# New turns for the head steps and group ends of the experts phase

## The reference

```python
h = x + _gqa(_rmsnorm(x, attn_norm_w), wq, wk, wv, wo)
out = h + _moe(_rmsnorm(h, ffn_norm_w), gate_w, expert_w)
# _moe: logits = t @ gate_w.T; w, sel = top_k(logits, 2); w = softmax(w)
#       comb = sum(w * one_hot(sel)); out = sum over 8 experts of comb[:, e] * (t @ expert_w[e].T)
# and behind it: x = x + _layernorm(out)
```

## Time and profile before

| | us |
|---|---|
| median of 3 runs | 711.88 (710.86 to 712.08) |
| profiled execution, in all | 706.54 |
| its span | 704.8 |
| experts phase in it | 586.5 to 704.8 |

### The profile page before, as it was taken

One profiled execution on the slowest core, in us unless ns is written; L12 is line 12 of the kernel. 1 busy time (PEld: TensorE's weight loads), 2 busy tenths in 40 slices (PEclk: granted clock), 3 DMA queues, 4 the chain that ended last, 5 costly groups with the idle time before them and its releaser, 6 DMA issues. The chain is left out here.

```text
span 704.8 us, 11736 instructions
## 1 busy us (share of the span) xinstructions
PE 560.1 (79%) x3810; PEld 312.0 (44%) x3810; DVE 524.4 (74%) x2234; ACT 359.0 (51%) x738; POOL 269.7 (38%) x467
## 2 busy tenths in 40 slices
PE   1966488568867998597999999999998988997670
PEld 1865377466656665112233333333334544553230
DVE  6599999442564777598899999999980552695986
ACT  5841045400202667102687887878877543445534
POOL 2001108700004467301445454454544542645564
PEclk9997565557995999655799999999999987998795
DMA  8000000000000184300111121111200000000001
GB/s 306 1 1 1 0 1 1 0 1 0 1 1 1 57 245 147 112 0 7 29 35 36 29 62 30 35 35 29 63 2 7 1 1 2 0 15 16 15 30 45
DMA packets 17579, 24.76 MB, mean 35 GB/s; under 512 B 3246, under 2 KB 14014, under 8 KB 17342
## 3 DMA queue, kind: packets, MB, share of 16 engines
q1 hardware_dynamic: 16942, 21.91, 10.1%
q10 hardware_dynamic: 576, 2.10, 0.9%
HBM read 13.65 MB, written 10.35 MB: 34 GB/s over the span
## 5 line engine op out<-in xcount | busy, mean ns | idle before, releaser
L1422 DVE CUSTOM_DVE_ANT_0 d_masked_S<-d_pS,d_wide_mask 128x512 bf16<-128x512 f32 (+3 forms) x512 | 217.0, 485 | 15.2 <-PE d_pS L1546 10.2
L1520 ACT ACTIVATE d_P<-d_pT 128x768 f32<-128x768 f32 (+1 forms) x192 | 165.9, 882 | 62.8 <-PE d_pT L1546 61.3
L1390 POOL TENSOR_SCALAR_AFFINE_SELECT d_P<-d_P 128x256 f32<-128x256 f32 x256 | 102.6, 415 | 133.9 <-ACT d_P L1520 133.9
L1546 PE MATMUL d_pS<-Ks,Qs 48*128 48x512 bf16 (+3 forms) x512 | 109.9, 332 | 19.7 <-DVE d_mx L1422 9.0
L1546 PE MATMUL d_pO<-d_P,V 128*32 128x512 f32 (+3 forms) x1024 | 99.2, 463 | 1.4 <-POOL d_P L1390 0.9
L1546 PE MATMUL d_pT<-Qs,Ks 51*128 51x512 bf16 (+3 forms) x512 | 72.3, 310 | 2.0 <-ACT d_mT L1490 2.0
L1546 PEld LDWEIGHTS d_pS<-Ks,Qs 48*128 48x128 bf16 x512 | 34.8, 97 | 72.1 <-DVE d_mx L1422 62.2
L1895 PE MATMUL e_PE<-gate_expT,w_qkvT 128*128 128x512 f32 x96 | 52.4, 698 | 7.1 <-DVE e_T L1764 3.3
L1546 PEld LDWEIGHTS d_pT<-Qs,Ks 51*128 51x128 bf16 x512 | 20.7, 94 | 73.8 <-ACT d_P L1520 42.3
L1422 DVE DVE_READ_ACCUMULATOR2_ANT d_mx<- 128x1 f32 x512 | 42.3, 83 | 0.0
L1739 POOL TENSOR_TENSOR e_T<-e_T 128x512 f32<-128x512 f32 x16 | 20.3, 1267 | 44.2 <-ACT e_T L1872 28.5
(11 more groups left out here) (312 smaller groups left out, 1092.3 us busy)
## 6 DMA issues: line engine op xcount, KB each, us to landing
Qs<-q_stack SPq DMA_DIRECT2D x32, 192.0 KB, 3.0
q_stack<-Qp SPq DMA_DIRECT2D x8, 384.0 KB, 2.6
X<-in_x_dram ACTq DMA_DIRECT2D x4, 512.0 KB, 6.3
q_stack<-Qp SPq DMA_DIRECT2D x8, 256.0 KB, 2.5
out_dram<-e_moe SPq DMA_DIRECT2D x8, 256.0 KB, 2.0
w_qkvT<-in_w_qkvT_dram SPq DMA_DIRECT2D x1, 1536.0 KB
Ks<-k_stack SPq DMA_DIRECT2D x32, 48.0 KB, 3.2
q_stack<-Qp SPq DMA_DIRECT2D x8, 128.0 KB, 2.1
```

The lines of the kernel that those rows point to most:

```text
L1390: last = nc.gpsimd.affine_select(out=view, in_=view, compare_op=ALU.is_ge, fill=0.0, base=0, pattern=[[0, 2], [1, 128]], channel_multiplie ...
L1422: last = nc.vector.tensor_tensor_reduce(out=out_[:, at:at + w], in0=src[:, at:at + w], in1=wide_mask[:, 512 - w:512], scale=1.0, scalar=LO ...
L1520: nc.scalar.activation(P[pair % 4][:, :, P_AT[unit]:P_AT[unit] + w], pT[(3 * pair + unit) % 2][:, :, 0:w], ACT.Exp, scale=float(HD4) ** -0 ...
L1546: return nc.tensor.matmul(out, lhsT, rhs, start=start, stop=stop)
```

## The change

The turns of the phase are set anew. Each of the two chunks gets a place of its own (1 and 12) in the place of eight turns a chunk, and the head steps get other distances. In turns counted from the phase's start:

| step | chunk 2 before, after | chunk 3 before, after |
|---|---|---|
| transposes of the attention | 2, 1 | 10, 12 |
| projection | 3, 4 | 11, 15 |
| residual | 4, 4 | 12, 15 |
| mean square | 5, 5 | 13, 16 |
| inverse root | 6, 6 | 14, 17 |
| transposes of h | 6, 7 | 14, 18 |
| gate | 7, 10 | 15, 21 |
| choice | 9, 9 | 17, 20 |
| exponential | 10, 11 | 18, 22 |
| weights | 11, 12 | 19, 23 |

At a group's end total and deviation stay in turns 4g + 6 and 4g + 7. VectorE's shift, now called `scalars`, goes from 4g + 8 to 4g + 9, ScalarE's normalising from 4g + 8 to 4g + 11, GpSimd's finish from 4g + 10 to 4g + 13. No instruction is added or taken away.

```diff
-        PE_STEPS = {-14: "attention_by_channel", -13: "project", -10: "h_by_channel", -9: "gate"}
-        DVE_STEPS = {-12: "residual", -7: "choose", -5: "weigh"}
-        ACT_STEPS = {-14: "attention_by_channel", -11: "mean_square", -10: "h_by_channel", -6: "exp_difference"}
-        POOL_STEPS = {-10: "inverse_root"}
-        GROUP_TURNS = {"total": 6, "deviation": 7, "normalise": 8, "finish": 10}
-        TURNS = range(TILES + 7)
+        HEAD_AT = {2: 1, 3: 12}
+        PE_STEPS = {0: "attention_by_channel", 3: "project", 6: "h_by_channel", 9: "gate"}
+        DVE_STEPS = {3: "residual", 8: "choose", 11: "weigh"}
+        ACT_STEPS = {0: "attention_by_channel", 4: "mean_square", 6: "h_by_channel", 10: "exp_difference"}
+        POOL_STEPS = {5: "inverse_root"}
+        GROUP_TURNS = {"total": 6, "deviation": 7, "scalars": 9, "normalise": 11, "finish": 13}
+        TURNS = range(TILES + 10)
 
         def due(u, steps):
 
-            return [(steps[u - CT * c], c) for c in chunks if u - CT * c in steps and (c >= EARLY or u >= CT * c)]
+            return [(steps[u - at], c) for c, at in HEAD_AT.items() if u - at in steps]
...
-                def normalise(g):
+                def scalars(g):
...
-                    for g in group_due(u, "normalise"):
-                        normalise(g)
+                    for g in group_due(u, "scalars"):
+                        scalars(g)
                         if g == LAST:
                             dve.wait_ge(sm["out"], LAST)
                             finish_last()
```

## The result

| | before | after |
|---|---|---|
| median of the runs, us | 711.41 (710.86 to 712.08) | 701.85 (700.78 to 704.04) |
| span of the profiled execution | 704.8 | 700.6 |
| experts phase in it (start, length) | 586.51, 118.3 | 590.91, 109.7 |

The ratio of the times is 0.9869, 95% interval 0.9842 to 0.9896: 1.3% faster, 9.6 us between the medians. The forecast was 705.0 us.

A forecast was written before the change was run, and what follows sets the result against it. It took the bound to alternate: a chain through ScalarE's wait where heads run, almost VectorE alone in the tail. Tile 30 at 679.9, work ending 694.9 and a 3.0 store gave span 697.9; 711.88 - 6.9 = 705.0 us, range 699.5 to 710.0.

The forecast's parts named there:

- The walk: Experts phase in the new order, laid out on VectorE's scale starts with prices and waits; span 697.9, 6.9 us less.
- the blocking between tiles 16 and 24: VectorE held by GpSimd in this stretch: pair 2.3, choosing 1.0, weighing 1.2, two totals 0.5, so 5.0 us.
- the pair of group 2: VectorE's two small scalar instructions for that group, claimed blocked beside GpSimd's root and a finish, 2.3 us.
- both readings of the root: Whether GpSimd's root blocks VectorE at group 2's pair: taken as blocked; the opposite reading would be 1.6 us lower.
- the reason for the gain before tile 16: Normalising two turns behind its scalars never waits and chunk 3's steps hang on nothing late; 8.1 us won.
- The group in the tail: Steady state after the head steps: 10.6 us a group against 11.4, with ScalarE's wait gone and VectorE full.
- The 3.7 us at tile 4: Projection now follows tile 4, so VectorE's scale of it comes 3.7 us earlier, 599.0 instead of 602.76.
- the waits at the residual and at tile 6: VectorE waits 1.6 us for chunk 2's projection, then 1.3 us while TensorE does tiles 5 and 6.
- the longer end: After the last statistics, group 6's normalising and finish follow the last deviation: 4.6 us where before took 2.6.
- A: VectorE's scalar pairs: none of three blocked, or each once only; 3 to 6 us more, about 700.5; chance 0.18.
- B: Gates one turn behind choosing, TensorE at 1.2 GHz adding 3.6 us at chunk 2, 1.2 at chunk 3: 709.8; chance 0.14.
- C: TensorE's clock held at 1.2 GHz from tile 12 on, as tiles come singly: span 714, 721 us; chance 0.08.

The follow-up runs named there:

- e_groups: The changed kernel with the head steps in their turns of before, so only the group ends have new turns; phase 112.2 us, ratio to before 0.990.
- e_heads: The changed kernel with the group ends as in before, so only the head steps have new turns; phase 110.0 us, ratio to before 0.991.
- e_norm_same_turn: The changed kernel with ScalarE's normalising in the turn of the shift (4g + 9, not 4g + 11); phase 108.4 us, ratio to before 0.984.
- e_project_early: The changed kernel with both projections one turn earlier (3 and 14), ahead of tiles 4 and 15; phase 110.3 us, ratio to before 0.988.
- e_order: The changed kernel with the normalising of group 6 ahead of the last deviation in ScalarE's program; phase 108.3 us, ratio to before 0.988.
- e_slot: The changed kernel with GpSimd's finish of groups 0 to 5 in turn 4g + 15, ahead of the next deviation; phase 105.8 us, ratio to before 0.983.
- the narrow finish: The changed kernel with GpSimd's finish adding one of 128 columns, output incomplete; phase 104.1 us, timed median 696.59 us in one run.

## Why the prediction was right, and where it was not

**The time.** 705.0 was forecast, 701.85 measured, inside the range. In the phase the working gave 6.9 us less and the traces show 8.6; the other 1.0 of the 9.6 us between the medians lies in the phases ahead or in the noise of the timed runs. Of the 3.2 us by which the forecast is too high, 1.7 are from the phase, 0.5 from the median of before (711.88 was taken, 711.41 measured) and 1.0 is that remainder.

**The walk, by its own anchors** (on before's clock): tile 4 at 599.0, measured 599.27; tile 16 at 637.9, 638.48; tile 24 at 664.0, 662.62; tile 30 at 679.9, 678.25; last statistics 10.4 us behind that, 10.4; end 4.6, 4.6; store 3.0, 3.0. The list of VectorE's instructions with their prices was the right way to size it, since VectorE was the bound after the change: idle 0.7 us between tiles 16 and 30. The residual waited 1.42 us for the projection and tile 6 1.27 (1.6 and 1.3 in the walk).

**The term that was mis-sized** is the blocking between tiles 16 and 24, 5.0 us in the walk. It came to 3.4. 2.3 of the 5.0 were the pair of group 2 beside GpSimd's root and a finish. The root does not block: 0.15 and 0.16 us at 645.93, and the finish came after them. Against that choosing was blocked for 1.8 us, not 1.0 (L1164 1.04 in place of 0.17, the two of L1172 1.31 in place of 0.36). Weighing (1.0) and the two totals (0.3 each) were near what the walk had. The stage took 24.1 us in place of 26.1. The prediction had both readings of the root and took the wrong one. The Trainium skill ("SBUF — State Buffer", "Who interferes with whom") says that a VectorE instruction with two SBUF inputs contends with a GpSimd instruction that reads SBUF; the trace does not agree for this one, 0.15 and 0.16 us beside the root. From tile 24 to 30, 15.6 us against 15.9 in the walk: both pairs met a finish and an addition, as said.

**The step that was wrong is the reason for the gain before tile 16.** For the kernel before, the prediction read the hole rightly: e_groups leaves the heads where they were, takes ScalarE's wait away, and the hole shrinks from 7.48 to 1.2 us. But I said that the changed kernel gains there since the normalising is two turns behind and never waits. That is not needed: e_heads has the wait (32.1 us) and no hole; e_norm_same_turn has it (27.4 us) and is faster than the changed kernel. Once the squares and the copy of chunk 3 did not stand right behind the wait and right ahead of tile 16's gate, it was a place where ScalarE had nothing urgent to do. The hole needed both: the wait ahead and the short distance behind. Either half of the change removes it, and so the parts do not add up (8.3 and 6.1 to 8.6). e_groups moves the shift, the normalising and the finish together, so that which of its turns takes the wait out of the way was not tried. The walk was of the whole change, and for the whole its places came out; the reason that stood beside it was never put to a sum of its own, and that the number is right is luck as far as the reason goes.

**The group in the tail** came out as the walk had it (10.6 us in place of 11.4; 10.67 and 11.37 measured), but "the wait on ScalarE goes" is not needed for it either: e_norm_same_turn has 10.67 with that wait. In before, as in e_heads (11.38), VectorE idles three times in this group for GpSimd, 0.8 us together: before two sums and before the shift (0.35 us). In the changed kernel and in e_norm_same_turn it does not idle there. These two have the shift one turn later and the finish three; which of the two does it was not tried.

**The 3.7 us at tile 4** were right as a place (3.5 measured) and are hardly a gain: e_project_early gives them back and loses 0.6 us, since TensorE has the same to do up to tile 6. I had named them as won there, though the walk gives 2.9 of them back as the waits at the residual and at tile 6.

**The order at the end costs 1.3 to 1.4 us.** The prediction saw the longer end (4.6 for 2.6 us) but not that it could be had without: e_norm_same_turn, which drops the lag, and e_order, which keeps it and only puts the normalising ahead of the last deviation, take 1.3 and 1.4 us off. So it is the place behind the deviation that costs, not the lag.

**Rivals.** A (pairs unblocked) held for one of three pairs. B did not come: no idle time of VectorE stands before either choosing; the 1.58 us before the sum ahead of the first one are the wait for GpSimd's addition, 1.7 in the walk. C did not come: TensorE idles up to 2.4 us between tiles, as in before (up to 3.4), and the slow clock shows in part (four tiles in 8.83 us at 668.30, granted clock 0.81; in before 9.10 us at 0.78 from 666.87 and 7.13 at 1.00 from 678.25), but the granted clock of the stages is 0.94, 0.93 and 0.89, and no scale of VectorE behind tile 6 waits for a tile. The terms that the prediction gives for C add up to a span of 713 us, not 714.

## What to carry to other kernels

When one engine will be the bound after a change, add up that engine's instructions between fixed points in the new order, with what blocks them; that gave each of five places within 1.7 us. The longest wait of an idle engine is no cause by itself: ask what stands behind it and when that is needed, and test the two halves of a change apart, since either may be enough. A reading of the kernel before can be right and still not be the reason why a change gains. Small VectorE instructions beside GpSimd's additions are worth placing: moving the finishes, 1.26 us each, into GpSimd's idle time was worth 3.9 us here.

## What was not expected of the hardware

GpSimd's power instruction (1.65 us for 128x8, 1.02 for 128x4) does not block a VectorE instruction with two SBUF inputs, while its 128x512 addition of 1.26 us does. Nor does the root of 128x8 block VectorE's addition of 128x512 (0.68 us in e_groups), so the size of VectorE's instruction is not the reason. Whether it is the kind of GpSimd's operation or the few elements that it reads was not tried; the narrow finish (128x4) is over in 0.20 us, too short to tell. The profile is also rough in the spans of GpSimd's instructions. A VectorE tensor_scalar on 128x8 with one input tensor was blocked too, 0.97 us beside an addition. The Trainium skill, "SBUF — State Buffer", "Who interferes with whom", lets tensor_scalar contend in a 2-port mode; the trace agrees that it can be held up (0.97 us); whether it was in such a mode no run here shows.

Which of the two waits at a meeting depends on who is first: in e_slot GpSimd's finish took 1.72 us since VectorE's waiting total went in ahead of it, while in the changed kernel VectorE's second instruction came 0.1 us after GpSimd's next one (670.87 behind 670.78, 681.54 behind 681.45) and waited for all of it.
